# First cross attention: one run of float32r matmuls per slot, queries and keys two slots ahead

## What is computed

```python
q = (hidden_states @ Wq).reshape(B, Sq, H, D)          # layernorm(x), 16 heads of 128
k = (encoder_hidden_states @ Wk).reshape(B, Skv, H, D) # context, 128 x 128 per batch
v = (encoder_hidden_states @ Wv).reshape(B, Skv, H, D)
q, k = rmsnorm(q, gq), rmsnorm(k, gk)
scores = jnp.einsum('bqhd,bkhd->bhqk', q, k) * scale
attn = jax.nn.softmax(scores, axis=-1)
out = jnp.einsum('bhqk,bkhd->bqhd', attn, v).reshape(B, Sq, H * D)
x = x + out @ Wo
```

## Time and profile before

| | us |
|---|---|
| median of three runs | 1745.27 |
| the profiled execution, its own time | 1747.42 |
| its span, first to last instruction | 1745.6 |
| the stage of the change (first cross attention), about | 243 to 693 |
| busy over the span: PE / weight loads / DVE / ACT / POOL | 1584.3 / 1268.7 / 1103.5 / 844.4 / 736.9 |
| mean granted TensorE clock | 0.966 |

### The profile page before, as it was taken

One profiled execution on the slowest core, in us unless ns is written; L12 is line 12 of the kernel. 1 busy time (PEld: TensorE's weight loads), 2 busy tenths in 40 slices (PEclk: granted clock), 3 DMA queues, 4 the chain that ended last, 5 costly groups with the idle time before them and its releaser, 6 DMA issues. The chain is left out here.

```text
span 1745.6 us, 33313 instructions
## 1 busy us (share of the span) xinstructions
PE 1584.3 (91%) x10768; PEld 1268.7 (73%) x10768; DVE 1103.5 (63%) x2458; ACT 844.4 (48%) x2326; POOL 736.9 (42%) x908
## 2 busy tenths in 40 slices
PE   4999969999999998999968988889999999878887
PEld 1556658888888886888845555479999999766776
DVE  3566647777777775555445565545556555589996
ACT  1344437777777776322224444445555555432221
POOL 3576715555455553232222222103333333357775
PEclk8999979999999999999979999989999999999998
DMA  5000020000000000000030000020000000000000
GB/s 220 1 0 0 0 85 3 4 2 3 3 2 3 3 2 21 1 1 1 1 121 1 0 0 0 1 88 8 8 7 7 6 4 2 1 3 13 9 12 13
DMA packets 15401, 28.74 MB, mean 16 GB/s; under 512 B 1489, under 2 KB 11986, under 8 KB 14546
## 3 DMA queue, kind: packets, MB, share of 16 engines
q1 hardware_dynamic: 15314, 27.63, 4.4%
HBM read 25.53 MB, written 2.10 MB: 16 GB/s over the span
## 5 line engine op out<-in xcount | busy, mean ns | idle before, releaser
L1272 POOL TENSOR_TENSOR weights_even<-weights_even,cross_reciprocal 128x512 f32<-128x512 f32 x64 | 67.0, 1047 | 256.5 <-DVE cross_reciprocal L1390 256.5
L845 POOL TENSOR_TENSOR weights_odd_early<-weights_odd_early,cross_reciprocal 128x512 f32<-128x512 f32 x64 | 66.6, 1040 | 199.0 <-DVE cross_reciprocal L976 199.0
L1317 ACT ACTIVATE weights_even<-bank,cross_shift 128x128 f32<-128x128 f32 x256 | 90.5, 366 | 102.0 <-DVE cross_shift L1382 102.0
L1039 PEld LDWEIGHTS bank<-ident,weights_odd_early 128*128 128x128 f32 x768 | 94.4, 142 | 44.8 <-issue 32.8
L1039 PE MATMUL bank<-ident,weights_odd_early 128*128 128x128 f32 x768 | 116.1, 274 | 1.7 <-DVE weights_odd_early L959 1.2
L2060 DVE TENSOR_REDUCE grouped_maxima<-bank 128x4 bf16<-128x512 f32 x128 | 82.3, 685 | 54.9 <-PE bank L2126 54.8
L885 ACT ACTIVATE weights_odd_early<-bank,cross_shift,cross_q_rms 128x128 f32<-128x128 f32 x256 | 113.5, 455 | 2.2 <-DVE cross_shift L953 2.2
L1974 ACT ACTIVATE grouped_probs<-bank 128x512 f32<-128x512 f32 x128 | 67.6, 600 | 84.9 <-PE bank L2144 84.9
L1611 POOL TENSOR_TENSOR mlp_low_inner<-mlp_inner,mlp_high_inner 128x512 fp32r<-128x512 f32 x36 | 48.4, 1345 | 125.9 <-ACT mlp_high_inner L1652 125.9
L1380 DVE TENSOR_REDUCE cross_maxima<-bank 128x4 f32<-128x512 f32 x64 | 44.2, 690 | 82.1 <-PE bank L1487 81.9
L367 POOL TENSOR_TENSOR causal_masked_maxima<-causal_maxima,causal_constants 128x512 bf16<-128x512 bf16 x64 | 67.7, 1079 | 63.2 <-DVE causal_maxima L492 63.1
(11 more groups left out here) (305 smaller groups left out, 5354.6 us busy)
## 6 DMA issues: line engine op xcount, KB each, us to landing
weights_odd_early<-in_weights SPq DMA_DIRECT2D x2, 3072.0 KB, 13.7
weights_even<-in_weights SPq DMA_DIRECT2D x2, 2560.0 KB, 11.9
weights_even<-in_weights SPq DMA_DIRECT2D x2, 1732.0 KB, 8.9
weights_odd_late<-in_weights SPq DMA_DIRECT2D x2, 1536.0 KB, 8.6
x<-in_x SPq DMA_DIRECT2D x4, 512.0 KB, 5.8
out<-mx_result SPq DMA_DIRECT2D x16, 128.0 KB, 1.7
weights_even<-in_weights SPq DMA_DIRECT2D x2, 512.0 KB, 8.7
cross_context<-in_context SPq DMA_DIRECT2D x16, 64.0 KB, 1.8
```

The source lines that it names most:

```text
L1039: last = pe.transpose(bank[:, j * P:(j + 1) * P], source, core.ident[:, :])
L1272: pool.tensor_tensor(probs[x], probs[x], reciprocal[x][:, :].unsqueeze(2).to_broadcast([P, JOBS, P]), ALU.mult).then_inc(probs_divided, 1)
L1317: last = act.activation(probs[x][:, j, :], bank_scores[x][:, j * P:(j + 1) * P], ACT.Exp, scale=SCALE, bias=shift[x][:, j:j + 1], accum_ou ...
```

## The change

The orders of the four engines in a slot are rewritten. PE: `turn_q(i+1)` goes ahead of the scores; `add_output(i-2)`, `project_q(i+2)` (one slot earlier than before) and `project_k(i+2)` stand in one run; `turn_k(i+1)` and `weigh_context(i-1)` end the slot. ACT: the high heads (now of group i-2), `square_q` and `copy_qT` open the slot and `copy_kT` closes it. DVE: `sum_k(i+1)` moves from the end of slot i-1 to behind the low heads of slot i, `copy_q` is one slot earlier, `update_x` goes from g = 2 to g = 1. POOL: `rms_of_k(i+1)` goes from the end of slot i-1 to the head of slot i. SP is not touched.

```diff
--- before.py
+++ after.py
@@ -848,12 +848,12 @@
             def step(t, s):
                 for g in range(GROUPS):
                     i = GROUPS * t + g
+                    if there(i + 1):
+                        rms_of_k(i + 1, (g + 1) % 2)
                     if there(i):
                         divide(i, g % 2)
                     if there(i + 1):
                         rms_of_q(i + 1, (g + 1) % 2)
-                    if there(i + 2):
-                        rms_of_k(i + 2, g % 2)
                     if g == 3 and batch_there(t - 1):
                         layer.pool_rstd(pool, t - 1, STATISTICS_STEPS)
             batches_in_turn(pool, step)
@@ -915,21 +915,21 @@
             def step(t, s):
                 for g in range(GROUPS):
                     i = GROUPS * t + g
+                    if there(i - 2):
+                        copy_high_heads(i - 2, g % 2)
+                    if there(i + 1):
+                        square_q(i + 1)
+                        copy_qT(i + 1, (g + 1) % 2)
                     if g == 1 and batch_there(t + 1):
                         copy_high(t + 1, 1 - s)
                     if there(i - 1):
                         copy_probsT(i - 1, (g - 1) % 2)
                     if there(i):
                         exponentials(i, g % 2)
-                    if there(i + 1):
-                        square_q(i + 1)
-                        copy_kT(i + 1, (g + 1) % 2)
                     if there(i + 2):
                         square_k(i + 2)
                     if there(i + 1):
-                        copy_qT(i + 1, (g + 1) % 2)
-                    if there(i - 1):
-                        copy_high_heads(i - 1, (g - 1) % 2)
+                        copy_kT(i + 1, (g + 1) % 2)
             batches_in_turn(act, step)
 
         @block.vector
@@ -1000,21 +1000,21 @@
                     i = GROUPS * t + g
                     if there(i - 2):
                         make_low_heads(i - 2, g % 2)
+                    if there(i + 1):
+                        sum_k(i + 1, (g + 1) % 2)
                     if there(i):
                         row_maxima(i, g % 2)
                     if g == 1 and batch_there(t + 1):
                         make_low(t + 1, 1 - s)
                     if there(i + 1):
                         scale_k(i + 1, (g + 1) % 2)
-                        copy_q(i + 1)
+                        sum_q(i + 1, (g + 1) % 2)
                     if there(i):
                         reciprocals(i, g % 2)
-                    if there(i + 1):
-                        sum_q(i + 1, (g + 1) % 2)
-                    if g == 2 and batch_there(t - 1):
+                    if there(i + 2):
+                        copy_q(i + 2)
+                    if g == 1 and batch_there(t - 1):
                         update_x(t - 1)
-                    if there(i + 2):
-                        sum_k(i + 2, g % 2)
                     if g == 0 and batch_there(t + 1):
                         layer.dve_normalise(dve, t + 1)
                     if g == 2 and batch_there(t - 1):
@@ -1112,28 +1112,26 @@
                 for g in range(GROUPS):
                     i = GROUPS * t + g
                     b0, s0, g0 = t + (g - 1) // GROUPS, (s + (g - 1) // GROUPS) % 2, (g - 1) % GROUPS
-                    b1, s1, g1 = t + (g + 1) // GROUPS, (s + (g + 1) // GROUPS) % 2, (g + 1) % GROUPS
                     b2, s2, g2 = t + (g + 2) // GROUPS, (s + (g + 2) // GROUPS) % 2, (g + 2) % GROUPS
                     b3, s3, g3 = t + (g - 2) // GROUPS, (s + (g - 2) // GROUPS) % 2, (g - 2) % GROUPS
                     turned_h = t + 1 if g == 1 and batch_there(t + 1) else None
+                    if there(i + 1):
+                        turn_q(i + 1)
                     if there(i):
                         scores(i, g % 2)
                     if turned_h is not None:
                         turn_h(t + 1, 1 - s)
                     if there(i - 1):
                         turn_probs(i - 1, g0 % 2)
+                    if there(i - 2):
+                        add_output(i - 2, g3 % 2, b3, s3, g3)
+                    if there(i + 2):
+                        project_q(i + 2, b2, s2, g2)
+                        project_k(i + 2, b2, s2, g2)
                     if there(i + 1):
-                        project_q(i + 1, b1, s1, g1)
+                        turn_k(i + 1, turned_h)
                     if there(i - 1):
                         weigh_context(i - 1, g0 % 2, s0)
-                    if there(i + 1):
-                        turn_k(i + 1, turned_h)
-                    if there(i + 2):
-                        project_k(i + 2, b2, s2, g2)
-                    if there(i + 1):
-                        turn_q(i + 1)
-                    if there(i - 2):
-                        add_output(i - 2, g3 % 2, b3, s3, g3)
             batches_in_turn(pe, step)
```

## The result

The changed kernel takes 1750.82 us in the median of nine runs (1748.68 to 1757.68), the kernel before 1745.61 in nine: a ratio of 1.0034, 95% interval 1.0021 to 1.0048. It is slower by 5.2 us (3.7 to 8.4 by the interval) where 4.1 had been forecast, and 1750.8 lies in the range of 1743 to 1755. The profiled execution took 1749.87 us with a span of 1748.0.

What follows compares the result with a forecast made beforehand. PE's queue was taken to bound the first cross attention. The terms -7.4, -1.1, +12.9 and -0.3 sum to +4.1 us on 1745.27, giving 1749.4 us, range 1743 to 1755.

Steps and rivals of the forecast that it cites:

- Term 1: On PE, add_output's wait for update_x where a batch begins, 0.50 us lost 15 times, goes: -7.4 us.
- Term of the regrouping: On PE, float32r runs go from three in a slot to one, 8 ns per entry saved: -1.1 us, bounds 0 and 11.
- rival B: On PE, each entry into a float32r run really costs 0.085 us, so grouping gains 11 us: 1739.5 us; chance 0.05.
- Terms 2 to 4: The heads chain, k chain and keys across ACT, DVE and POOL fit with 0.07, 0.15 and 0.1 to 0.2 spare: cost 0.
- Term 5: On SP, the context load is issued later, so PE stands 0.92 us before turn_h in 14 batches: +12.9 us.
- Term 6: At the stage's ends, later first scores, shorter early waits and an unhidden softmax chain: -0.3 us, bounds -3 and +3.
- A: The context load on SP arrives in time for turn_h or costs little: 1736.5 us; chance 0.06.
- C: The heads chain through ACT and DVE does not fit its 0.07 spare: +4.7 to +12 us, 1754 to 1761; chance 0.13.
- D: PE's longest stretch without float32r, 3.4 us, runs at half clock in each of 15 batches: 1800 us; chance 0.02.

Runs made afterwards that it cites:

- `update_x` alone: The kernel before with only update_x moved to g = 1, as the last thing of DVE's slot, and nothing regrouped: 1738.98 us, ratio 0.9958.
- own buffers: The changed kernel with the context that turn_h reads loaded by a separate DMA into two further buffers: 1741.88 us, ratio 0.9971 to the kernel before.
- two runs: The changed kernel with separate buffers and load for the turned context, project_k behind turn_k and copy_kT ahead of square_k: 1738.40 us, ratio 0.9958.
- squares first: The changed kernel with separate buffers and load for the turned context, and square_q ahead of copy_high_heads on ACT: 1752.55 us, ratio 1.0030.
- old order with a late load: The kernel before with one more wait on SP, so a context's load is issued at the end of the slot: 1764.35 us, ratio 1.0104.

## Why the prediction was right

**The bound.** PE's queue bounds the stage: the three orders without either wait come to 400.5 to 400.9 us for the 60 slots, with one, two or three float32r runs in a slot.

**Term 1, the wait for `update_x`.** Forecast -7.4 for 15 waits; `update_x` alone took 7.0 off the 60 slots, which hold 14 of them (14 x 0.49 = 6.9).

**Term of the regrouping.** Forecast -1.1, bounds 0 and 11. It is nothing: ordinary slots have 6.60 us with three runs, 6.59 with two and 6.61 with one. Against the forecast gain of 1.1 us, one run costs some 0.2 to 0.3 us more than three over the 60 slots: the sign was wrong, which mattered little. That the 11 us of rival B are not there is shown twice, by `update_x` alone against own buffers (400.6 against 400.9) and by two runs against one. Where the 10 to 20 ns between these orders lie was not followed up.

**Terms 2 to 4, the chains at no cost.** They fit: with the load's wait gone (own buffers) PE's recorded waits lie only in the first two and the last slots, and none between is for heads, keys or maxima. Of the heads chain even the spare was right to 0.01: squares first puts the loop at 6.53, against slots of 6.61.

**Term 5, SP's queue.** Forecast +12.9 (14 x 0.92); the 14 turn_h slots grew by 12.6, and own buffers took 12.5 off again. The old order with a late load makes the same wait from the other side. This is the term that turned a gain of 8 us into a loss, and it lies in a queue that the diff does not touch.

**Term 6, the ends.** Forecast -0.3. First scores 0.9 later, slots 0 and 1 shorter by 1.45, the last slot by 1.8 (0.5 of it the fifteenth wait, counted above), the tail 0.9 longer: -0.95.

**Sum.** 12.6 (turn_h slots) - 7.0 (14 waits) + 0.2 (6.61 for 6.60) - 1.4 (ends, with the fifteenth wait) = 4.4, as the stage measured. The two large terms were right to 0.3 us (term 5) and 0.1 (term 1, 7.5 for all 15 waits). That the errors of the two small ones partly cancel is luck: the regrouping came out 1.3 us worse than forecast, the ends 0.65 better. The medians are 5.2 apart; the interval of the ratio covers both.

**The rivals.** A (the context in time): refuted by the wait itself. B: above. C (heads chain): not in the changed kernel, and squares first shows what it costs once the chain is 0.29 late. D (the clock): the granted clock stayed at 1.00 from 253 to 690 us, although in the turn_h slots the stretch without float32r is now 3.4 us of work and more than 4 with the standing (the prediction has the standing inside the 3.4). The Trainium skill's page "TensorE: Matmul & The Clock Gate", section "Part 4: PE-mode transpose", has it that transposes do not count as activity. This trace does not contradict it (float32 matmuls stand among the transposes), but nothing in this stage follows from it.

## What to carry to other kernels

When a piece of work is moved within a slot, list who waits for its semaphore on every queue, the DMA queue too: a load whose issue hangs on the moved matmul moves with it, and its time from release to landing (here mostly 1.85 to 2.1 us from the end of the weighing, once 3.45) has to fit ahead of its reader. Price a change of matmul type over the whole stretch between two equal points, not by the first matmul of the new type, whose longer pitch is given back by the short one ahead. And before regrouping an engine that is dense, look for the one wait per batch: here moving `update_x` alone brought all that there was to gain in the slots (400.6 us for the 60).

## What the runs showed that was not expected

- A float32r run in its first matmul shows 0.32 us to the next where the following show 0.235 (512 columns), in each order; the transposes ahead show 0.35 for four in place of 0.44. Together they cost what the parts cost elsewhere, to within 10 ns in the earlier trace rows and in the run of two.
- The 14 loads of the kernel before landed 1.84 to 2.36 us behind the recorded end of the weighing, those of the changed kernel 1.88 to 2.10. Over all nine profiles 157 of 168 context loads in this stage took 1.66 to 1.97 us from issue to landing and eleven took 2.06 to 3.67. The kernel before had spare for its one such load (2.18); an order that leaves no spare pays for each of them on PE. The Trainium skill's page "DMA: Bandwidth & Descriptors", section "Anatomy of one DMA", has a fixed cost of about 2.0 us for each DMA on another issue path. With 0.17 us to the issue and 1.7 to 1.8 behind it, the usual one here is close to that.
- Layers whose code is the same differed between profiles by up to 8.5 us in sum (1292.3 to 1300.8). Half of it is the grouped attention: 259.3 to 261.2 us at a granted clock of 0.94 to 0.95 in five profiles, 263.5 to 264.3 at 0.92 to 0.93 in the four with the longest rest. Differences of 3 us between these kernels are not told apart by their medians, but well by their slots.
